# Storing the spread queries of the maxima by patch, head and query

## The reference

```python
x = x + _L0_conv_ref(_gn(x), L0_conv_W)
x = x + _L1_conv_ref(_gn(x), ...)
# _L1_conv_ref: 16 heads of 8 channels, a 7 x 7 window of keys around each query
qkv = (x @ w_qkv + b_qkv).reshape(B, H, W, 3, HEADS, HEAD_DIM)
logits.append(jnp.einsum('bnhwd,bnhwd->bnhw', q, ks) + bias[None])   # 49 times
attn = jax.nn.softmax(logits, axis=-1)
return out @ w_proj + b_proj
```

## Time and profile before

| | before |
|---|---|
| median of 2 runs | 1424.5 us (1421.59 to 1427.41) |
| the profiled execution | 1432.87 us, of which the span is 1431.1 us |
| TensorE matmul busy | 1158.9 us (81%) |
| TensorE weight load busy | 811.7 us (57%) |
| VectorE busy | 880.3 us (62%) |
| ScalarE busy | 674.5 us (47%) |
| GpSimd busy | 593.9 us (42%) |
| mean granted clock of TensorE | 0.859 of full speed |

### The profile page before, as it was taken

The page is one execution under the profiler, slowest core; times in us unless marked ns, Lnnn a source line. Parts: engine busy times, 40 slices in busy tenths (PEclk is TensorE's granted clock), DMA queues, the critical chain, the costliest instruction groups (busy, mean ns, idle before and its releaser), DMA issues.

```text
span 1431.1 us, 38250 instructions
## 1 busy us (share of the span) xinstructions
PE 1158.9 (81%) x12441; PEld 811.7 (57%) x12441; DVE 880.3 (62%) x2129; ACT 674.5 (47%) x1867; POOL 593.9 (42%) x1278
## 2 busy tenths in 40 slices
PE   3799998556888788778979887888789788879882
PEld 3455555444666556556656664666556566656661
DVE  3422222696777576667757674767577676757671
ACT  2100000703565556565746655565557465655651
POOL 3000000500746455454636462646455454637461
PEclk7799999556899897889989997999888889989996
DMA  9200000241547374645555464657375554645472
GB/s 253 56 35 34 34 34 34 74 99 20 144 103 177 80 179 104 140 113 125 144 107 142 101 161 76 156 100 171 82 181 127 113 141 96 157 98 144 98 179 51
DMA packets 142497, 159.57 MB, mean 112 GB/s; under 512 B 29952, under 2 KB 119888, under 8 KB 142040
## 3 DMA queue, kind: packets, MB, share of 16 engines
q1 hardware_dynamic: 141432, 153.13, 45.3%
q0 software_dynamic: 864, 3.90, 0.8%
HBM read 86.09 MB, written 70.47 MB: 109 GB/s over the span
## 4 chain that ended last, share of the span: by engine, by line
PE 53%; DMA 26%; DVE 9%; issue 6%; SPq 4%; ACT 0%; POOL 0%; DVEq 0%; POOLq 0%; ACTq 0%
DMA area<-mcol 22%; PE PS L1080 13%; PE PS L1185 11%; PE PS L1148 9%; PE PS L1169 5%; PE PS L1092 4%; PE PS L1162 3%; DVE bias L933 3%; PE PS L1133 3%; PE PS L1195 3%; DVE area L975 2%; DMA area<-x 2%; SPq L423 1%; SPq L444 1%; DVE mcol L986 1%
## 5 line engine op out<-in xcount | busy, mean ns | idle before, releaser
L570 POOL TENSOR_TENSOR halves<-masked 128x96 f32<-128x96 f32 (+1 forms) x512 | 203.5, 397 | 493.3 <-DVE masked L1007 492.7
L1148 PE MATMUL PS<-area 97*128 97x48 bf16 (+1 forms) x4112 | 257.8, 211 | 138.9 <-DMA area<-mcol 119.7
L996 DVE TENSOR_TENSOR S<-PS,bias 128x384 f32<-128x384 f32 (+1 forms) x513 | 283.9, 554 | 121.2 <-PE PS L1148 115.9
L746 ACT ACTIVATE VT<-PS 128x128 f32<-128x128 f32 x449 | 126.2, 281 | 418.2 <-PE PS L1133 416.0
L1185 PE MATMUL PS<-S,VT 128*64 128x96 f32 (+1 forms) x4096 | 310.5, 278 | 0.0
L1148 PEld LDWEIGHTS PS<-area 97*128 97x128 bf16 x4112 | 186.6, 105 | 217.2 <-issue 158.9
L753 ACT ACTIVATE S<-S 128x384 f32<-128x384 f32 (+1 forms) x512 | 274.7, 539 | 46.5 <-DVE S L996 33.3
L1185 PEld LDWEIGHTS PS<-S,VT 128*64 128x64 f32 x4096 | 207.1, 148 | 143.5 <-issue 91.7
L1007 DVE TENSOR_TENSOR masked<-PS,cst 128x192 f32<-128x192 f32 (+1 forms) x512 | 181.6, 355 | 101.2 <-PE PS L1185 95.2
L986 DVE TENSOR_REDUCE mcol<-PS 128x6 bf16<-128x480 f32 (+2 forms) x297 | 181.5, 611 | 96.2 <-PE PS L1169 96.1
L1080 PE MATMUL PS<-area 128*128 128x392 f32 x576 | 192.0, 496 | 3.9 <-DVE area L875 3.9
(11 more groups left out here) (87 smaller groups left out, 1142.3 us busy)
## 6 DMA issues: line engine op xcount, KB each, us to landing
k_parts<-area SPq DMA_DIRECT2D x204, 168.0 KB, 4.1
area<-k_parts SPq DMA_DIRECT2D x33, 1008.0 KB, 8.3
q_parts<-area SPq DMA_DIRECT2D x204, 98.0 KB, 2.3
area<-q_parts SPq DMA_DIRECT2D x66, 294.0 KB, 5.9
xa<-x_mid SPq DMA_DIRECT2D x18, 392.0 KB, 6.6
late<-x_mid SPq DMA_DIRECT2D x17, 392.0 KB, 8.8
out<-area SPq DMA_DIRECT2D x17, 392.0 KB, 8.5
den<-sums SPq DMA_DIRECT2D x66, 98.0 KB
```

The source lines that it names most:

```text
L570: nc.gpsimd.tensor_tensor(h, m[:, :, 0:2, :], m[:, :, 2:4, :], ALU.add).then_inc(s["half"], 1)
L996: nc.vector.tensor_tensor(S[:, n % 4, 0:cols], PS[:, SCORE + n % 2, 0:cols], bias[:, at:at + cols], ALU.add).then_inc(s["biased"], 1)
L1148: last = mm(PS[:, SCORE + n % 2, cols * g:cols * (g + 1)], key_rows[a][0:PEAK_ROW + 1, g, key:key + 128], query_rows[a][0:PEAK_ROW + 1, g, ...
```

## The change

`Qbd` is stored as patch, head, query instead of head, query, patch. It has the same size and the same place. A spread still writes 392 elements of one head, now as 49 runs of 8 (one run for each patch, 128 elements apart), and it reads `qparts[0]` in that order, so that neighbouring elements of the read lie 49 elements (98 bytes) apart. The 128 stationary columns of a patch matmul were 49 elements apart and are one run now.

```diff
-        Qbd = part(1, 0, 3136, BF16).rearrange("p (h q t) -> p h q t", h=HEADS, q=PATCH)
+        Qbd = part(1, 0, 3136, BF16).rearrange("p (t h q) -> p t h q", h=HEADS, q=PATCH)
...
                 for h in heads:
-                    last = nc.scalar.activation(Qbd[:, h, :, :], qparts[0].rearrange("p (a q t) -> p a q t", a=2, q=PATCH)[:, c % 2],
+                    last = nc.scalar.activation(Qbd[:, :, h, :], qparts[0].rearrange("p (a q t) -> p a t q", a=2, q=PATCH)[:, c % 2],
                                                 ACT.Copy, scale=cst[:, C_HEAD + h:C_HEAD + h + 1])
...
                 for h in heads:
-                    last = nc.vector.tensor_scalar(Qbd[:, h, :, :], qparts[0].rearrange(
-                        "p (a q t) -> p a q t", a=2, q=PATCH)[:, c % 2], cst[:, C_HEAD + h:C_HEAD + h + 1], None, ALU.mult)
+                    last = nc.vector.tensor_scalar(Qbd[:, :, h, :], qparts[0].rearrange(
+                        "p (a q t) -> p a t q", a=2, q=PATCH)[:, c % 2], cst[:, C_HEAD + h:C_HEAD + h + 1], None, ALU.mult)
...
-                queries = Qbd.rearrange("p h q t -> p (h q) t")
+                queries = Qbd.rearrange("p t h q -> p t (h q)")
...
-                    last = mm(PS[:, PEAK, PATCH_KEYS * i:PATCH_KEYS * (i + 1)], queries[:, :, first + i],
+                    last = mm(PS[:, PEAK, PATCH_KEYS * i:PATCH_KEYS * (i + 1)], queries[:, first + i, :],
```

## The result

The changed kernel takes 1533.78 us (median of two runs, 1530.55 to 1537.0) against 1424.5 us before: the ratio on record is 1.0738, with a 95% interval from 1.0668 to 1.0807. It is slower by 109 us by the medians and by 7.4%, or 105 us, by the ratio, where 2.9% (+40 us) was forecast. The direction was right and the size was not. The measured time lies inside the stated range of 1418 to 1545, but outside the forecast's own 1440 to 1500: only the price set on a rival (one stream, 1542) took the range that far.

What follows compares the result with a forecast made beforehand. TensorE carried 53% of the chain, and time lost between its restart and the first patch bank was lost once per chunk. 51.5 + 3.4 - 14.6 = +40 us gave 1465 us; range 1418 to 1545.

Steps and rivals of the forecast that it cites:

- one stream: Rival, chance 0.22: VectorE's spreads read one element at a time with jumps, each growing 0.63 us; +117 us, 1542 us.
- The path: Per chunk, time lost from TensorE's restart after the maxima to its first patch bank counts once; VectorE's longer spreads add +51.5 us.
- the restart: Point in each chunk where TensorE resumes after waiting for the row of maxima, 12.78 us from issue to landing.
- step 3: Point in each chunk where TensorE begins the nine banks of patch scores, behind VectorE's spreads.
- 60 us or so foretold: Sign: TensorE waits for VectorE's L975 at L1162 in all 32 chunks, 60 us or so in place of 9.5.
- 0.31 us: Growth of each VectorE spread (L975) from far reads, middle of 0.24 to 0.39; +51.5 us in the loop, +3.4 in the prologue.
- costed at nothing: ScalarE's spreads (L736): 0.15 us longer each, covered by ScalarE's 0.42 us wait for VectorE; without that cover 10 us.
- -14.6 us: Patch matmuls (L1169) with side-by-side weights: 0.019 us gained on each of 24 per chunk, over 32 chunks.
- free jumps: Rival, chance 0.28: jumps cost VectorE's reads nothing, so each spread grows by 0.115 us; +1 us, 1426 us.
- the weights win: Rival, chance 0.05: patch matmuls drop to 0.033 us and all 48 of a chunk count, -40 us; 1400 us.
- do nothing at the matmul: Rival, no separate chance: a strided weight load costs the same as a packed one, so no gain; +55, 1480 us.

## Why the prediction was wrong

- **The path.** Right. What is lost between the restart and step 3 is lost once per chunk. TensorE waits for L975 at L1162 in 32 chunks (18 cases before), and near reads on VectorE alone take 74 us off the changed kernel. The wait there came to 36.8 us and not to the 60 or so foretold: another 35.2 us (0.9 before) stand one step earlier, at L1148 behind VectorE's bias add L996. Together they grew by 62 us.
- **The price of a spread on VectorE** (term "0.31 us"). It was 0.37, in the stated 0.24 to 0.39. Put into the same sum, 6 x 0.37 = 2.22 and 0.36 + 1.85 - 0.37 = 1.84, mean 2.03, times 32 = 65 us, and 4 for the prologue: 65 + 4 - (51.5 + 3.4) = 14 us above the forecast. The mechanism held; whether the elements go in two streams at 2.5 ns a step or in one at 1.2 is not counted by any run.
- **The price on ScalarE** ("costed at nothing"). The row it was taken from, L651, was a poor neighbour: the estimate was 0.15 us, the far read costs 0.60. With near reads on VectorE 14 us of it were not covered. With far ones, as in the changed kernel, no loss from it shows; the nothing came out about right there with a wrong price.
- **TensorE's clock.** The step that failed. The sum took every later instruction at the duration it had before. But the longer waits let the granted clock fall to half, and TensorE does its first banks there: 21 of 32 chunks against one. From the first bank to the reciprocal that costs 53 us where it cost 3, so 50 us stood at nothing in the sum. Work in the wait gives at least 35 us back. No term and no rival had this.
- **The weights** (term "-14.6 us"). Right at the full clock: six in 0.41 us against 0.43 said, and 15 us over the stretches. At the half clock there is no gain: six take 0.61 us in the prologue before the change and 0.61 behind the wait after it.

Together: 40 forecast, 14 for the longer spreads and 50 for the clock are 104 us, and the two profiled executions differ by 1535.2 - 1431.1 = 104.1 us (109 by the medians). The traces divide it in the same way: 36 us lie between the first banks and the reciprocals (50 for the clock less 15 for the weights, rounded), 3 ahead of the first bank of all, and the other 65 where the sum with 0.37 us puts 65. That it comes out so exactly is in part luck: the median times have an uncertainty of some 10 us, and the parts can feed each other.

The rivals: free jumps are out, by 6.70 us in the prologue against 3.9. One stream at the prices it was given (a growth of 0.63 us, over 9 us in the prologue) is out too; at its lowest price, 1.17 ns an element, it would grow by 0.34 us, and that is not told from the measured 0.37 by length. Its 1542 us lie near the 1534 measured by luck, since they rest on a growth of 0.63. That the weights win, or do nothing at the matmul, is out as well.

## What to carry to other kernels

A store that suits one reader is paid for by each writer: count the instructions on both sides, and their start-to-start times in an unhurried stretch such as a prologue, before turning a layout. When a change makes TensorE wait longer, price the work behind the wait at the half clock too, and not only the wait: here that was 50 of 104 us. A few throwaway matmuls placed in the wait tell in one run whether the clock is a part of a loss (35 us here, a lower bound, since they cost time themselves); where the wait is short they only cost (38 us).

## What the runs showed of the hardware

- An element-by-element jump costs by engine and by side. ScalarE: 4 bytes nothing (613 ns for 392 elements), reads at 98 bytes 1210, writes at 256 bytes 2072. VectorE: reads at 4 bytes 0.529 us from start to start and at 98 bytes 0.604, against 0.325 for near reads, all written in 49 runs, and 0.234 for one run throughout; writes at 256 bytes take at least 1182 ns each.
- 49 runs of 8 against one run of 392: 407 ns on VectorE, all between 400 and 418 with GpSimd at work beside them. 50 runs against one of 400: 319 ns, and up to 977.
- A weight load of 128 bf16 columns 98 bytes apart lasts 163 ns in the median, side by side 98, and the matmuls behind it go at 0.041 instead of 0.059 us at the full clock.
- TensorE's granted clock can be at half behind stalls that are short and have work between them: 0.50 at 862 us, behind stalls of 1.33 and 1.03 us. 21 of 32 first banks of the change began so, and 6 of 32 with four 480-column matmuls placed in the second wait.
